# Last stage of a graph and feed-forward block: one chunk less in flight, and a magnitude copy moved to ScalarE

## The reference

```
xn = layernorm(x)
g  = GATv2(rmsnorm(xn) @ W_down, edges; Wl, Wr, att) @ W_up       # 4 heads of 64
m  = linear_attention(xn; Wq, Wk, Wv, biases) @ Wo + bo           # 16 heads of 64
x1 = x + g + m
t  = quant(layernorm(x1))                                         # NVFP4, blocks of 16
hid = silu(t @ quant(gate_w).T) * (t @ quant(up_w).T)             # 512 wide
out = x1 + quant(hid) @ quant(down_w).T
```

## Time and profile before

| | |
|---|---|
| median of 3 runs | 1178.48 us (1175.84 to 1181.55) |
| profiled execution | 1182.05 us, its span 1180.3 us |
| busy in the span | TensorE 1022.6, VectorE 861.1, ScalarE 627.5, GpSimd 394.6 us |
| last stage | from 924 us to 1180.3 us |

### The profile page before, as it was taken

One profiled execution on the slowest core, in us unless ns is written; L12 is line 12 of the kernel. 1 busy time (PEld: TensorE's weight loads), 2 busy tenths in 40 slices (PEclk: granted clock), 3 DMA queues, 4 the chain that ended last, 5 costly groups with the idle time before them and its releaser, 6 DMA issues. The chain is left out here.

```text
span 1180.3 us, 16636 instructions
## 1 busy us (share of the span) xinstructions
PE 1022.6 (87%) x5061; PEld 817.0 (69%) x5061; DVE 861.1 (73%) x1456; ACT 627.5 (53%) x1391; POOL 394.6 (33%) x393
## 2 busy tenths in 40 slices
PE   2697489998989989998999579999999977999984
PEld 1686389897988979888998337888888533445532
DVE  5874177677676767677777979888986578887786
ACT  3263246556455556555555348888888324423431
POOL 0213756676666676666663000000000100000000
PEclk9798789899989999998999769999999988999987
DMA  9254767877786786767774358898988263433323
GB/s 245 29 186 122 218 193 242 242 237 235 215 252 211 229 255 216 235 214 224 219 230 141 118 184 248 290 275 270 266 254 247 93 137 82 102 78 75 82 33 55
DMA packets 108860, 220.65 MB, mean 187 GB/s; under 512 B 25197, under 2 KB 57542, under 8 KB 108666
## 3 DMA queue, kind: packets, MB, share of 16 engines
q1 hardware_dynamic: 87349, 154.24, 39.9%
q0 software_dynamic: 19920, 55.84, 21.1%
q10 hardware_dynamic: 1508, 9.52, 2.4%
HBM read 157.60 MB, written 72.50 MB: 195 GB/s over the span
## 5 line engine op out<-in xcount | busy, mean ns | idle before, releaser
L985 POOL DMA_INDIRECT score_gath<-xl_rows,misc x324 | 347.6, 1073 | 178.1 <-issue 102.5
L1025 PE MATMUL score_ps_m<-x_hi,score_w_hi 128*128 128x416 f32 (+1 forms) x576 | 215.1, 373 | 14.9 <-issue 8.9
L1157 DVE TENSOR_TENSOR score_zb<-score_gath,score_ps_x 128x1024 f32<-128x1024 f32 x81 | 98.7, 1219 | 167.5 <-remote 136.0
L1027 PE MATMUL score_ps_m<-x_hi,score_w_lo 128*128 128x416 f32 (+1 forms) x576 | 209.1, 363 | 12.6 <-issue 12.5
L1026 PE MATMUL score_ps_m<-x_lo,score_w_hi 128*128 128x416 f32 (+1 forms) x576 | 209.8, 364 | 10.9 <-issue 10.8
L1621 PE MATMUL ps_all<-agg_gath,agg_hot 128*125 128x256 f32 x648 | 181.6, 417 | 0.3 <-DVE agg_hot L1728 0.2
L1673 ACT ACTIVATE agg_gath<-agg_gath,prob 128x64 f32<-128x64 f32 x648 | 158.8, 341 | 7.1 <-DMA agg_gath<-edge_rows 6.7
L1025 PEld LDWEIGHTS score_ps_m<-x_hi,score_w_hi 128*128 128x128 f32 x576 | 113.2, 197 | 22.1 <-issue 19.2
L1027 PEld LDWEIGHTS score_ps_m<-x_hi,score_w_lo 128*128 128x128 f32 x576 | 112.6, 196 | 18.1 <-issue 16.1
L1026 PEld LDWEIGHTS score_ps_m<-x_lo,score_w_hi 128*128 128x128 f32 x576 | 113.3, 197 | 15.7 <-issue 14.5
L1621 PEld LDWEIGHTS ps_all<-agg_gath,agg_hot 128*125 128x125 f32 x648 | 100.1, 190 | 28.7 <-issue 21.0
(11 more groups left out here) (318 smaller groups left out, 1610.1 us busy)
## 6 DMA issues: line engine op xcount, KB each, us to landing
edge_rows<-score_gath SPq DMA_DIRECT2D x81, 520.0 KB
agg_gath<-edge_rows SPq DMA_DIRECT2D x81, 520.0 KB, 5.2
local_bc<-local_rows SPq DMA_DIRECT2D x40, 224.0 KB
score_gath<-xl_rows,misc POOLq DMA_INDIRECT x324
xb_rows<-in_x ACTq DMA_DIRECT2D x1, 5000.0 KB, 20.1
phi_c<-phi_rows SPq DMA_DIRECT2D x10, 500.0 KB, 4.0
xb_rows<-in_L_mix_bo POOLq DMA_DIRECT2D x10, 500.0 KB, 7.5
x_bo<-xb_rows SPq DMA_DIRECT2D x10, 500.0 KB
```

What stands on the lines that cost most here:

```text
L985: nc.gpsimd.indirect_dma_start(out=gath[:, g % GS, q, :], out_offset=None, in_=xl_rows, in_offset=bass.IndirectOffsetOnAxis(ap=src_idx[:, ...
L1025: pe.matmul(acc, w_hi[:, i % 2, kk, :], x_hi[:, kk, cols], start=(kk == 0), stop=False)
L1027: mm = pe.matmul(acc, w_lo[:, i % 2, kk, :], x_hi[:, kk, cols], start=False, stop=(kk == KC - 1))
L1157: v.tensor_tensor(zb[:, u, :].rearrange("p (q d) -> p q d", q=GP), gath[:, g % GS, :, 0:HID], ps_x[:, u, :, :].rearrange("p h (q d) -> p ( ...
```

## The change

VectorE now takes chunks in the order `residual(c)`, `scale_of(c)`, `clip_x(c)`, `hidden(c-1)`, `quantise_x(c)`, `quantise_h(c-1)`. `clip_x` is `scales`, the product with the inverse scale and the clip. The two VectorE instructions that made the magnitude of x in bf16 (L1790, L1791) are replaced for x by one ScalarE instruction, `size(c)`: Abs with scale COARSE. For h they stay (`sizes`).

TensorE does, in each round from c = 1, `projections(c)` with `turn_x(c-1)` before the last `gnn_part`, `gates(c-1)`, and `down(c-2)`. `turn_h(b-1)` stands between the two halves of `gates(b)`. ScalarE does `copy_x(c-1)`, `deviation(c)`, `copy_h(c-2)`, `normalise(c)`, `gate(c-1)`, `result(c-2)`, `size(c)`. `deviation` begins with a Sqrt of one column of `eps` that isn't used for anything, ahead of its wait. `gate` waits for the gate half of the products alone, and `hidden` for both.

```diff
--- before.py
+++ after.py
@@ -1779,16 +1779,24 @@
         q.do(v.tensor_scalar(t, sc8, 2.0 ** -20, -1.0, ALU.max, ALU.mult))
         q.do(v.reciprocal(inv, t))
 
-    def rounded(self, x, width):
+    def clipped(self, x, width):
 
         v, q = self.v, self.q
         nb = width // 16
-        a, b = self.work[0:C, 0:width], self.coarse[0:C, 0:width]
+        a = self.work[0:C, 0:width]
         blocks = lambda ap: ap.rearrange("p (n s) -> p n s", s=16)
         q.do(v.tensor_tensor(blocks(a), blocks(x), self.small[0:C, 3, 0:nb].unsqueeze(2).to_broadcast([C, nb, 16]), ALU.mult))
         q.do(v.tensor_scalar(a, a, 6.0, -6.0, ALU.min, ALU.max))
+
+    def sizes(self, width):
+
+        v, q, a, b = self.v, self.q, self.work[0:C, 0:width], self.coarse[0:C, 0:width]
         q.do(v.tensor_scalar(b, a, COARSE, None, ALU.mult))
         q.do(v.tensor_scalar(b.bitcast(I16), b.bitcast(I16), 0x7FFF, None, ALU.bitwise_and))
+
+    def rounded(self, width):
+
+        v, q, a, b = self.v, self.q, self.work[0:C, 0:width], self.coarse[0:C, 0:width]
         q.do(v.scalar_tensor_tensor(out=a, in0=b, scalar=COARSE, in1=a, op0=ALU.max, op1=ALU.add))
         q.do(v.scalar_tensor_tensor(out=a, in0=b, scalar=COARSE, in1=a, op0=ALU.max, op1=ALU.subtract))
 
@@ -1828,7 +1836,7 @@
         hq = sb("hq", [C, FF], BF16)
         hq_t = sb("hq_t", [P, FF // P, C], BF16)
         y = sb("y", [C, 2, D])
-        eps = sb("eps", [C, 1])
+        eps = sb("eps", [C, 2])
         root = sb("root", [C, 10])
         total, minus, spread, std, var, inv, newton, rstd, shift = (root[:, i:i + 1] for i in range(9))
 
@@ -1870,6 +1878,9 @@
         s_acc = [sem(f"s_acc{i}") for i in range(2)]
         s_v = sem("s_v")
         s_eps = sem("s_eps")
+        s_clip = sem("s_clip")
+        s_size = sem("s_size")
+        s_half_g = sem("s_half_g")
         s_den = sem("s_den")
         s_pself = sem("s_pself")
         s_own = sem("s_own")
@@ -1882,7 +1893,7 @@
 
         quant_x = RowQuantiser(nc.vector, None, amax, small, work, coarse)
         quant_h = RowQuantiser(nc.vector, None, hid_amax, hid_small, hid_work[:, 0, :], hid_work[:, 1, :].bitcast(BF16))
-        TUCKED, HEAD = 6, 4
+        HEAD = 4
 
 
         with nc.Block() as block:
@@ -1970,9 +1981,7 @@
                     if c == 1:
                         turn_gnn(6)
                         turn_gnn(7)
-                    if c >= TUCKED:
-                        turn_x(c - 1)
-                        turn_h(c - 3)
+                    turn_x(c - 1)
                     gnn_part(c, 1)
 
                 def turn_x(b):
@@ -2000,6 +2009,10 @@
                     for i in range(2):
                         for kk in range(KC):
                             m = pe.matmul(ps_g[0:C, i, :], xq_t[:, kk, :], k.gate_q[:, i, :, kk, :], start=(kk == 0), stop=(kk == KC - 1))
+                        if i == 0:
+                            m.then_inc(s_half_g, 1)
+                            if 0 < b < NC - 1:
+                                turn_h(b - 1)
                     m.then_inc(s_g, 1)
 
                 def down(b):
@@ -2027,20 +2040,11 @@
                     gnn_part(0, half)
                 for c in range(2, 4):
                     turn_gnn(c)
-                projections(1)
-                projections(2)
-                for b in range(2):
-                    turn_x(b)
-                    gates(b)
-                for c in range(3, NC):
+                for c in range(1, NC):
                     projections(c)
-                    if c < TUCKED:
-                        turn_x(c - 1)
-                        turn_h(c - 3)
                     gates(c - 1)
-                    down(c - 3)
-                turn_h(NC - 3)
-                down(NC - 3)
+                    if c >= 2:
+                        down(c - 2)
                 turn_x(NC - 1)
                 gates(NC - 1)
                 for b in (NC - 2, NC - 1):
@@ -2062,13 +2066,14 @@
                     act.activation(hq_t[:, :, :], ps_th[:, 0:FF // P, 0:C], ACT.Copy).then_inc(s_hqt, 1)
 
                 def deviation(c):
+                    act.activation(eps[:, 1:2], eps[:, 0:1], ACT.Sqrt)
                     act.wait_ge(s_mean, c + 1)
                     act.activation(square, x1[:, c % 3, :], ACT.Square, bias=minus, accum_out=spread).then_inc(s_root, 1)
                     act.wait_ge(s_root, 2 * c + 1)
-                    act.activation(std, spread, ACT.Sqrt, bias=eps[:, :], scale=1.0 / D).then_inc(s_root, 1)
+                    act.activation(std, spread, ACT.Sqrt, bias=eps[:, 0:1], scale=1.0 / D).then_inc(s_root, 1)
 
                 def gate(b):
-                    act.wait_ge(s_g, b + 1)
+                    act.wait_ge(s_half_g, b + 1)
                     if b:
                         act.wait_ge(s_hid, b)
                     act.activation(e[:, :], ps_g[0:C, 0, :], ACT.Silu, scale=fs[0:C, 5:6]).then_inc(s_e, 1)
@@ -2088,6 +2093,10 @@
                     act.wait_ge(s_gt, c + 1)
                     act.activation(k.gnn_t[:, :, c * C:(c + 1) * C], ps_gt.rearrange("p (h n) -> p h n", h=2),
                                    ACT.Copy).then_inc(s_gtc, 1)
+
+                def size(c):
+                    act.wait_ge(s_clip, c + 1)
+                    act.activation(coarse[0:C, :], work[0:C, 0:D], ACT.Abs, scale=COARSE).then_inc(s_size, 1)
 
                 act.wait_ge(s_eps, 1)
                 act.wait_ge(s_den, 1)
@@ -2100,23 +2109,20 @@
                 normalise(0)
                 copy_gnn(6)
                 copy_gnn(7)
-                deviation(1)
-                copy_gnn(8)
-                copy_gnn(9)
-                normalise(1)
-                copy_x(0)
-                gate(0)
-                for c in range(2, NC):
+                size(0)
+                for c in range(1, NC):
                     copy_x(c - 1)
-                    if c >= 3:
-                        copy_h(c - 3)
                     deviation(c)
+                    if c == 1:
+                        copy_gnn(8)
+                        copy_gnn(9)
+                    if c >= 2:
+                        copy_h(c - 2)
                     normalise(c)
                     gate(c - 1)
-                    if c >= 3:
-                        result(c - 3)
-                copy_h(NC - 3)
-                result(NC - 3)
+                    if c >= 2:
+                        result(c - 2)
+                    size(c)
                 copy_x(NC - 1)
                 gate(NC - 1)
                 copy_h(NC - 2)
@@ -2130,7 +2136,7 @@
             @block.vector
             def _(v):
                 own = Steps(v, s_v)
-                v.memset(eps[:, :], 1e-5).then_inc(s_eps, 1)
+                v.memset(eps[:, 0:1], 1e-5).then_inc(s_eps, 1)
                 es = k.self_score[:, :, :]
                 own.mark(v.tensor_copy(den[:, 0, :, :], extra[:, :, 9:13]))
                 own.mark(v.tensor_copy(den[:, 1, :, :], extra[:, :, 13:17]))
@@ -2200,10 +2206,15 @@
                     own.do(v.tensor_tensor(shift, minus, rstd, ALU.mult))
                     v.sem_inc(s_scale, 1)
 
-                def quantise_x(b):
+                def clip_x(b):
                     v.wait_ge(s_h, b + 1)
                     quant_x.scales(h, D)
-                    quant_x.rounded(h, D)
+                    quant_x.clipped(h, D)
+                    v.sem_inc(s_clip, 1)
+
+                def quantise_x(b):
+                    v.wait_ge(s_size, b + 1)
+                    quant_x.rounded(D)
                     if b:
                         v.wait_ge(s_tx, b)
                     own.do(quant_x.product(xq[:, :], D))
@@ -2211,12 +2222,16 @@
 
                 def hidden(b):
                     v.wait_ge(s_e, b + 1)
+                    v.wait_ge(s_g, b + 1)
                     own.do(v.scalar_tensor_tensor(out=hid[:, :], in0=ps_g[0:C, 1, :], scalar=fs[0:C, 6:7], in1=e[:, :],
                                                   op0=ALU.mult, op1=ALU.mult))
                     v.sem_inc(s_hid, 1)
 
                 def quantise_h(b):
-                    quant_h.rounded(hid[:, :], FF)
+                    quant_h.scales(hid[:, :], FF)
+                    quant_h.clipped(hid[:, :], FF)
+                    quant_h.sizes(FF)
+                    quant_h.rounded(FF)
                     if b:
                         v.wait_ge(s_th, b)
                     own.do(quant_h.product(hq[:, :], FF))
@@ -2228,23 +2243,20 @@
                 scale_of(0)
                 node_rows(6)
                 node_rows(7)
+                clip_x(0)
                 quantise_x(0)
-                residual(1)
-                node_rows(8)
-                node_rows(9)
-                scale_of(1)
-                quantise_x(1)
-                for c in range(2, NC):
-                    hidden(c - 2)
+                for c in range(1, NC):
                     residual(c)
-                    quant_h.scales(hid[:, :], FF)
+                    if c == 1:
```

(12 more changed lines are left out.)

## The result

Over 20 runs of each kernel the changed one takes 1185.47 us in the median (1175.51 to 1191.43), the one before 1178.05. The ratio is **1.0058**, 95% interval 1.0035 to 1.0082: about 6.8 us slower. The forecast was 1184.7, +6.2.

What follows compares the result with a forecast made beforehand. VectorE was taken to bound the early rounds, TensorE chunks 6 to 9, with latency at both ends. Terms +8.87, +1.23, +1.39, -1.38, +1.10 and -4.97 gave +6.2 on 1178.48: 1184.7 us, 8-in-10 range 1180 to 1190.

Steps and rivals of the forecast that it cites:

- Start: First chunks: tucked transposes and gates ahead of mix delay chunk 2's `residual` by 8.87 us.
- R2: Start of `residual` of chunk 2 on VectorE; forecast at 985.1 against 976.19 us.
- VectorE's rounds: Early rounds set by VectorE: 22.47 us against 21.24, since waits for ScalarE stand open.
- TensorE's rounds: Later rounds set by TensorE: 23.43 us, +0.37, as down waits for `copy_h` behind Square and root.
- R5 to R6: From `residual` of chunk 5 to chunk 6's: 1.38 us shorter, x transposes now being tucked in for every chunk.
- Table load: ScalarE's square root: dummy root takes a 1.28 us load off the chain; no further drain of about 1.38.
- The drain: From chunk 9's `residual` to the span's end: 4.97 us shorter, from one chunk less in flight.
- the 41 that the prediction had named as a sign of being wrong: After chunk 9's `residual`: a drain of over 41 us would show the prediction wrong.
- The total: Whole kernel: +6.2 us, a median of 1184.7 us.
- The rival of a falling clock: Early rounds: TensorE falls to its lower clock; +11.7 us, 1190.2; chance 13%.

Runs made afterwards that it cites:

- e1: Changed kernel with chunk 1's normalisation ahead of the two copies of the last graph transposes on ScalarE; ratio to the kernel before 1.0010.
- e2: As e1, plus chunk 0's x transposes moved behind chunk 1's last graph product; ratio to the kernel before 1.0020.
- e8: As e2, plus chunk 0's gate ahead of the last graph copies and those transposes ahead of chunk 2's mix; ratio to the kernel before 0.9993.
- e9: Kernel before, long order, with the change's savings, filled waits, early normalisation of chunk 1 and unused products in the drain; ratio to the kernel before 0.9965.
- e5: Changed kernel with h transposes ahead of both gate halves and their copy ahead of Square on ScalarE; ratio to the kernel before 1.0070.
- e3: Changed kernel without the extra square root; ratio to the kernel before 1.0145.
- e7: Kernel before with x transposes tucked ahead of the last graph product from chunk 5 instead of 6; ratio to the kernel before 0.9988.
- e4: Changed kernel with the magnitude of x made by VectorE again; ratio to the kernel before 1.0061.
- e6: Changed kernel with eleven and five unused products while TensorE waits for the last chunk's x and h; ratio to the kernel before 1.0052.

## Why the prediction was right, point by point

- **Start.** Said +8.87 at R2, measured +8.45. Both causes, the tucked transposes and the gates ahead of the mix, were shown (e1, e2, e8). What the forecast didn't name is that, with the transposes moved back (e2), slow gates(0) reach `hidden(0)` through ScalarE's queue.
- **VectorE's rounds.** Said 22.47, measured 22.35. The chain of rows added up; root to `normalise` is 1.54 for 1.62, and clip to L1800 1.19 for 1.26. e9 shows the other half of the argument: the same parts with the waits filled give 19.56.
- **TensorE's rounds.** Said 23.43, measured 23.36. `copy_h` starts 0.20 after the root does, not after its 0.30 have ended, so down starts at R + 3.72, not 3.84; the rest of the round is 0.05 longer than the sum had it. e5 takes the wait away, e3 lengthens it.
- **R5 to R6.** Said -1.38, measured -1.45; e7 gives the part by itself.
- **Table load.** +1.28 per round without the extra root (e3), in six intervals of two kinds to within 0.02. The 2.66 us per switch of the Trainium skill, "ScalarE: Activation LUTs", section "What ACT_TABLE_LOAD costs", isn't borne out here: 1.28 came back and not 2.66, and the measurement decides. Its statement that abs lies in every set ("Table sets: the hidden batching unit") agrees: no load stands before L2099.
- **The drain is the term that was mis-sized**: -4.97 said, -3.11 measured. At 41.25 us it also passes the 41 that the prediction had named as a sign of being wrong. I took 7.14 us for transposes, copy and gates from one execution, in which the clock rose among the gates. From the transposes to `hidden(9)` it is 7.25 in e4 and 9.07 in the changed kernel, whose lists differ in the magnitude alone. Of the 1.82 between them 1.46 is the gates' own time (5.01 and 6.47), by the clock; 0.35 lies between the end of the gates and `hidden(9)` (0.13 and 0.48), and no run shows why. A range of 0 to 1.9 belonged here, as I had given one for the start. In e6, with the upper clock held, the drain is 37.33.
- **The total** was right in part by luck: the drain came 1.86 longer than said, and the start, the rounds and R5 to R6 together 0.9 shorter, which leaves 7.19 for 6.24 in the stage.
- **The rival of a falling clock** (13%) came true in part, in some executions: R4 to R5 took 25.3 to 26.3 in e3, e5 and e6 (1.28 of e3's is its load) and 23.4 in e1, e2, e4 and e8. Against this rival the prediction held that its rows show a fall only at a 5 us wait; in e6 and the changed kernel one comes behind a wait of 2.37. From R2 to R5 e6 has the same lists as the changed kernel, whose profile shows the level down at the same place, but back within the down products, and 23.44 (window after the change, below). How much of the median +6.8 it holds over many executions stays open.

```profile
1021.00:1023.00 2.00, 2.00 (x6) 0.92 (x4) 0.46 (x3) 1.27 (x3) 0.00 (x0) 0.50 0.11 20
```

## What to carry to other kernels

Taking work off the engine that sets a round pays only if that engine has something to do while it waits for the answer; count the open waits of the new order before counting the instructions removed. Fewer stages in flight cost such fillers in every round and give back one drain. Write out the first and the last chunk by themselves: in in-order lists the position of one pair of copies was worth 4 us there, and a tuck that pays in the steady state cost 4.4 at the start.

## What the runs showed of the hardware

The granted clock of TensorE isn't the same from run to run at one place. With the same lists and waits of TensorE of 2.37 us ahead of it, the lower level (1.2 GHz) in chunk 4's round cost 1.9 us in e6 and 0.1 in the changed kernel's profile. Products that nobody reads held the upper level (2.4 GHz) through a 10 us wait (granted clock 1.00 in every window of e6 from 1156 to 1182): the drain is 37.33 us, against 39.97 to 41.25 in the changed kernel, e1, e2 and e8, whose drains have the same lists.
